# First stage of a convolution and mixture-of-experts kernel: the square root moved behind both product copies, exponentials two batches at a time, the first patches loaded before the stage ends, and half of a normalisation given to VectorE

## The reference, cut to what matters

```python
def branch(x, w, d):                       # four dilations d = 1, 4, 8, 12
    f = softmax(conv3x3(x, w, dilation=d), over the 9 outputs)      # (N, 9, H*W)
    return sum over the 9 taps k of  shifted(x, k, d) * f[k]        # per pixel
n = layernorm over channels of x           # x is (2, 256, 96, 96)
y = conv1x1(concat([n] + [branch(n, w, d) for w, d in ...]), w_proj) + b_proj
x = x + relu(group_norm(y))
t = layernorm(tokens of x)
x = x + t + top-2 mixture of 8 experts on t
```

## Time and profile before

| | us |
|---|---|
| median of 3 runs | 2487.01 (2482.56 to 2492.95) |
| the profiled execution, its own time | 2486.36 |
| its span, first to last instruction | 2484.5 |
| first stage, image 0 and image 1 | 281.9 and 271.6 |
| PE, DVE, ACT, POOL busy over the span | 1950.0, 1626.7, 1274.9, 1058.6 |

### The profile page before, as it was taken

How to read it: one execution, slowest core, us unless ns; L and a number is a source line. 1 busy time by engine, 2 the same in 40 slices (tenths; PEclk the granted TensorE clock), 3 DMA queues, 4 the chain that set the end, 5 groups by cost and what they waited for, 6 DMA issues and landing times.

```text
span 2484.5 us, 60548 instructions
## 1 busy us (share of the span) xinstructions
PE 1950.0 (78%) x20124; PEld 1843.4 (74%) x20125; DVE 1626.7 (65%) x4385; ACT 1274.9 (51%) x2717; POOL 1058.6 (43%) x1444
## 2 busy tenths in 40 slices
PE   4788699999968886999999928723999999993322
PEld 4677599999957775999999927723999999992222
DVE  3465465656555654777887848852788899894653
ACT  4566343333336663556666626512777777771211
POOL 2454412323225543146566614775555555551000
PEclk9999799999989997999999966556999999995555
DMA  5222155566632222677898787743666444446897
GB/s 135 82 77 77 50 177 149 139 173 169 167 107 83 77 64 86 194 208 241 254 269 263 232 277 250 249 162 128 197 207 192 155 159 162 153 157 212 294 302 252
DMA packets 334948, 433.66 MB, mean 175 GB/s; under 512 B 87469, under 2 KB 260141, under 8 KB 333805
## 3 DMA queue, kind: packets, MB, share of 16 engines
q1 hardware_dynamic: 260945, 294.85, 40.3%
q0 software_dynamic: 41024, 97.10, 11.1%
q10 hardware_dynamic: 32784, 39.07, 4.7%
HBM read 277.12 MB, written 159.94 MB: 176 GB/s over the span
## 4 chain that ended last, share of the span: by engine, by line
PE 47%; DMA 16%; DVE 12%; issue 9%; POOL 6%; ACT 6%; SPq 2%; DVEq 2%; POOLq 0%; ACTq 0%
PE ps_y L418 15%; PE ps L418 9%; DMA expert_out<-e_out,dest 6%; PE ps_a L418 6%; PE ps_o L992 6%; POOL expert_in L2204 5%; PE ps_b L929 4%; DMA o_acc<-res_scratch 3%; DMA o_y<-expert_out 3%; DVE stats L1568 2%; PE ps_x L1140 1%; PE ps_tok L831 1%; PE ps_a L875 1%; DVE rows_st L1630 1%; DVE cat_lo L1663 1%
## 5 line engine op out<-in xcount | busy, mean ns | idle before, releaser
L418 PE MATMUL ps_y<-cat_hi,wp 128*128 128x288 f32 x2048 | 473.7, 307 | 1.9 <-DVE cat_lo L1663 1.9
L2227 POOL DMA_INDIRECT expert_out<-e_out,dest x304 | 306.8, 1009 | 233.2 <-DMA expert_out<-e_out,dest 94.4
L2183 POOL DMA_DIRECT2D patches<-rows_scratch x352 | 196.8, 601 | 468.2 <-PE ps_o L979 262.4
L2141 POOL TENSOR_TENSOR taps<-taps,g_rows 96x108 f32<-96x108 f32 (+3 forms) x440 | 236.9, 566 | 271.5 <-ACT g_rows L1241 267.7
L418 PEld LDWEIGHTS ps_y<-cat_hi,wp 128*128 128x128 f32 x2048 | 346.4, 190 | 2.1 <-issue 1.1
L418 PE MATMUL ps_y<-cat_lo,wp 128*128 128x288 f32 x1024 | 303.8, 297 | 0.0
L1309 ACT ACTIVATE bands<-ps_b 112x288 f16<-112x288 f32 (+4 forms) x256 | 105.3, 411 | 342.9 <-PE ps_b L929 333.0
L1663 DVE SCALAR_TENSOR_TENSOR cat_lo<-ps_o,cat_hi 128x288 fp32r<-128x288 f32 (+1 forms) x576 | 227.3, 419 | 63.9 <-ACT cat_hi L1315 59.5
L1315 ACT ACTIVATE cat_hi<-ps_o 128x288 fp32r<-128x288 f32 (+1 forms) x576 | 212.9, 384 | 65.1 <-PE ps_o L979 30.6
L418 PE MATMUL ps<-e_hi,w_now 128*128 128x256 f32 x1216 | 242.6, 282 | 0.6 <-issue 0.2
L1655 DVE SCALAR_TENSOR_TENSOR bands<-ps_b,bands 112x288 f16<-112x288 f32 (+4 forms) x256 | 116.6, 455 | 191.4 <-ACT bands L1309 188.6
(11 more groups left out here) (241 smaller groups left out, 4939.1 us busy)
## 6 DMA issues: line engine op xcount, KB each, us to landing
e_x<-expert_in SPq DMA_DIRECT2D x152, 260.0 KB
o_y<-expert_out SPq DMA_DIRECT2D x48, 768.0 KB, 5.3
patches<-rows_scratch SPq DMA_DIRECT2D x160, 192.0 KB
patches<-rows_scratch SPq DMA_DIRECT2D x256, 108.0 KB
patches<-rows_scratch SPq DMA_DIRECT2D x192, 112.0 KB
x_in<-in_x SPq DMA_DIRECT2D x48, 384.0 KB, 3.2
rows_scratch<-rows_st SPq DMA_DIRECT2D x48, 384.0 KB, 3.0
y_scratch<-y_acc SPq DMA_DIRECT2D x48, 384.0 KB
```

The costliest lines, as they stand in the source:

```text
L418: mm = eng.matmul(out, lhs[p], rhs[q], start=start and n == 0, stop=stop and n == 2)
L2141: last = pool.tensor_tensor(here, here, g_rows[:, u, first:end, i, b:b + nb].rearrange("p r b k -> p r (b k)"), ALU.add)
L2183: pool.dma_start(patch_target(s, n), patch_source(m, s, n)).then_inc(patch_pooled[s % RING], 16)
L2227: pool.indirect_dma_start(out=ys_dram, out_offset=bass.IndirectOffsetOnAxis(ap=at, axis=0), in_=e_out[:, u, j], in_offset=None).then_inc(e ...
```

## The change

In the first stage, on all engines:

1. `deviation(k+2)` stands behind the copies of both taps 0 and 1.
2. The exponentials of batches b-1 and b are run together at the end of the step in which an odd b gets its logits (k = 10, 16, 22), in place in `f_low`. `weights(b-1)` follows in step k+1, `weights(b)` in step k+2, between `statistics` and the second part of `rows_st`; their transposes come one step later still (`weighed_in`, `turned_in`).
3. ACT normalises rows 0 and 1, DVE rows 2 and 3 (new `normalise` on DVE, signal `xn_more`), right after the first part of `rows_st`.
4. After step 23 PE makes both late taps ahead of the own products, with the transposes of batches 4 and 5 behind them.
5. SP and POOL issue the first patches after their last work of the first stage (`free_first_patches` waits until the memory under ring place 0 and the first 16 stored rows are ready).

```diff
+        def weighed_in(k):
+            b = summed_in(k - 1)
+            if b is not None and b % 2 == 1:
+                return b - 1
+            b = summed_in(k - 2)
+            return b if b is not None and b % 2 == 1 else None
         def turned_in(k):
-            return (k - 8) // 3 if k >= 8 and (k - 8) % 3 == 0 else None
+            return weighed_in(k - 1)
...
+        def free_first_patches(eng, m):
+            eng.wait_ge(tok_ready, (m + 1) * GROUPS)
+            eng.wait_ge(ch_ready, (m + 1) * GROUPS)
+            eng.wait_ge(rows_done, (m + 1) * GROUPS)
+            for u in range(2):
+                eng.wait_ge(rows_stored[u], 16 * (m * (GROUPS // 2) + 2))
+            eng.wait_ge(pads_zeroed, 16 * 4 * IMAGES)
...                                          # SP, before it leaves the first stage
+                free_first_patches(sp, m)
+                for n in range(loads(0)):
+                    if not second_queue(0, n):
+                        sp.dma_start(patch_target(0, n), patch_source(m, 0, n)).then_inc(patch_loaded[0], 16)
...                                          # PE
                     pe.wait_ge(xn_done, N + k + 1)
+                    pe.wait_ge(xn_more, N + k + 1)
...
-                late_products(GROUPS - 1)
+                tap_products(GROUPS - 1, 2)
+                tap_products(GROUPS - 1, 3)
+                for o in range(CC):
+                    own_products(GROUPS - 1, o)
+                    turn_filters(BATCHES - 4, o)
+                for o in range(CC):
+                    turn_filters(BATCHES - 3, o)
...                                          # ACT
-                    after(act, f_dve, 3 * (m * BATCHES + b))
-                    act.activation(f_pow[:], f_low[:, b % 2], ACT.Exp).then_inc(f_exp, 1)
+                    act.activation(f_low[:, b % 2], f_low[:, b % 2], ACT.Exp).then_inc(f_exp, 1)
...
                     if k + 1 < GROUPS:
-                        normalise(k + 1, (0, 1))
+                        normalise(k + 1)
                     if k:
                         late_products(k - 1)
-                    if k + 1 < GROUPS:
-                        normalise(k + 1, (2, 3))
                     keep_products(k, 0)
-                    if summed_in(k) is not None:
-                        exponentials(summed_in(k))
+                    keep_products(k, 1)
                     if k + 2 < GROUPS:
                         deviation(k + 2)
-                    keep_products(k, 1)
+                    if summed_in(k) is not None and summed_in(k) % 2 == 1:
+                        exponentials(summed_in(k) - 1)
+                        exponentials(summed_in(k))
...                                          # DVE
+                def normalise(k):
+                    dve.wait_ge(nmr_done, N + k + 1)
+                    for r in range(R // 2, R):
+                        last = dve.tensor_scalar(xn[:, k % 2, r], ps_tok[0:W, k % 2, r], rstd[0:W, k % 2, r:r + 1],
+                                                 nmr[0:W, k % 2, r:r + 1], ALU.mult, ALU.add)
+                    last.then_inc(xn_more, 1)
...
                     dve.wait_ge(xn_done, N + k + 1)
+                    dve.wait_ge(xn_more, N + k + 1)
                     dve.tensor_scalar(rows_st[:, u, :, 0], xn[:, u], SCALE, None, ALU.mult).then_inc(rows_hi_done, 1)
+                    if k + 1 < GROUPS:
+                        normalise(k + 1)
                     if summed_in(k) is not None:
                         lower(summed_in(k))
                     if k + 2 < GROUPS:
                         statistics(k + 2)
+                    if weighed_in(k) is not None:
+                        weights(weighed_in(k))
                     dve.wait_ge(rows_hi_done, N + k + 1)
                     dve.scalar_tensor_tensor(out=rows_st[:, u, :, 1], ...).then_inc(rows_done, 1)
                     if k + 2 < GROUPS:
                         factors(k + 2)
-                    if summed_in(k) is not None:
-                        weights(summed_in(k))
```

More of the change, by code:

```diff
@@ L470, in build @@
                 units += [("tap", m_, k_, 0), ("tap", m_, k_, 1)]
-            late_products(GROUPS - 1)
+            units += [("tap", m_, GROUPS - 1, 2), ("tap", m_, GROUPS - 1, 3)]
+            units += [("own", m_, GROUPS - 1, 0), ("turned", m_, BATCHES - 4, 0), ("own", m_, GROUPS - 1, 1), ("turned", m_, BATCHES - 4, 1)]
+            units += [("turned", m_, BATCHES - 3, 0), ("turned", m_, BATCHES - 3, 1)]
             units += [("logits", m_, BATCHES - 2), ("logits", m_, BATCHES - 1)]
@@ L702, in _ @@
                         kept += 1
-                    load_patches(s)
+                    if s:
+                        load_patches(s)
                     behind = s - UNITS1 - 18
@@ L1230, in normalise @@
                         act.wait_ge(rows_done, N + k - 1)
-                    for r in rows:
+                    for r in range(R // 2):
                         last = act.activation(xn[:, k % 2, r], ps_tok[0:W, k % 2, r], ACT.Identity,
                                               bias=nmr[0:W, k % 2, r:r + 1], scale=rstd[0:W, k % 2, r:r + 1])
-                    if R - 1 in rows:
-                        last.then_inc(xn_done, 1)
+                    last.then_inc(xn_done, 1)
                 def keep_products(k, r):
@@ L1277, in step @@
                     if k + 1 < GROUPS:
-                        normalise(k + 1, (0, 1))
+                        normalise(k + 1)
                     if k:
                         late_products(k - 1)
-                    if k + 1 < GROUPS:
-                        normalise(k + 1, (2, 3))
                     keep_products(k, 0)
-                    if summed_in(k) is not None:
-                        exponentials(summed_in(k))
+                    keep_products(k, 1)
                     if k + 2 < GROUPS:
                         deviation(k + 2)
-                    keep_products(k, 1)
+                    if summed_in(k) is not None and summed_in(k) % 2 == 1:
+                        exponentials(summed_in(k) - 1)
+                        exponentials(summed_in(k))
                 deviation(0)
                 deviation(1)
-                normalise(0, range(R))
+                normalise(0)
                 for k in range(GROUPS):
                     step(k)
-                late_products(GROUPS - 1)
+                keep_products(GROUPS - 1, 2)
+                keep_products(GROUPS - 1, 3)
+                for o in range(CC):
+                    keep_own(GROUPS - 1, o)
+                    keep_filters(BATCHES - 4, o)
+                for o in range(CC):
+                    keep_filters(BATCHES - 3, o)
                 exponentials(BATCHES - 2)
@@ L1642, in _ @@
                     step(k)
+                weights(BATCHES - 3)
                 lower(BATCHES - 2)
@@ L2159, in _ @@
                     add(2, 0, 1).then_inc(taps_added, 1)
+                free_first_patches(pool, m)
+                for n in range(loads(0)):
+                    if second_queue(0, n):
+                        pool.dma_start(patch_target(0, n), patch_source(m, 0, n)).then_inc(patch_pooled[0], 16)
                 leave(pool)
@@ L2177, in _ @@
                 thirds = 0
-                for s in range(STEPS):
+                for s in range(1, STEPS):
                     shared = [n for n in range(loads(s)) if second_queue(s, n)]
```

11 lines of the change are left out of this document (4 added, 7 removed).

## The result

| | before | after |
|---|---|---|
| median of 6 runs, us | 2487.55 (2482.56 to 2494.75) | 2507.75 (2504.77 to 2508.81) |
| the profiled execution, its own time | 2486.36 | 2504.77 |
| its span | 2484.5 | 2502.9 |

The changed kernel takes 1.0077 times as long (95% interval 1.0059 to 1.0096): slower by 0.77%. Forecast were 2493.4 us, a range of 2476 to 2510, and "within 0.5%" as the likeliest case. The time is in the range, 14 us above the value, and on the side (slower by over 0.5%) that I had given 0.23.

The account below looks back on a forecast made before the run. The prediction took a loop of waits between engines, not one engine, as the bound. From 2486.4 us, loop with clock +24.6, behind step 23 -9.0 and patches -8.6 gave 2493.4 us, range 2476 to 2510.

Parts of the forecast that it names:

- within 0.5%: Whole kernel: measured time between 2474.6 and 2499.4 us, hardly told from no change; given 0.65.
- The bound: First stage: no engine bounds it; a loop of waits between engines does, 8.71 us in a plain step.
- The steps without the clock: Loop, steps 7 to 23: +6.3 us an image without clock; steps 10 to 13 about 12.9, 8.8, 12.3, 15.0.
- Late square root, part 3: Loop steps: moving the square root and giving DVE half of the normalisation each change the time by 0.
- `weights`: DVE, steps 11, 12, 17, 18: now inside the loop, delaying `nmr` by 2.69 us each, +10.8 an image.
- The clock: PE behind seven long stalls: clock falls at 1.35 us each, less two before; +6 an image, bounds -2.7 and +16.2.
- two of before: PE in the old loop: clock falls behind two of five double stalls an image, subtracted from the seven expected.
- rival C: PE's products after the seven stalls: clock stays low for most of a step, +20.4, 2513.8 us; chance 0.13.
- Rival B: Loop as forecast, but PE's clock stays up as often as before: 2481.4 us; chance 0.20.
- Behind step 23: End of the first stage: last tap and POOL's additions come earlier, -4.5 us an image, bounds -1.0 and -7.5.
- Patches: Start of the second stage: PE's waits for first patches mostly go, -8.6 us together, bounds 0 and -9.7.
- Rival D: Start of the second stage: prefetch wins nothing, strip 1 being as late as strip 0 was; +8.6, 2502 us; chance 0.05.

Follow-up runs that it names:

- E9: Changed kernel, `weights` ahead of `statistics`, each exponential a step later behind an own-product copy, second part of `rows_st` ahead of `weights` and `statistics`: 2439.87 us, ratio 0.9790 to before.
- E10: Kernel before with parts 3 and 5 and the second part of `rows_st` ahead of the statistics: 2472.11 us, ratio 0.9923.
- E4: Changed kernel with small filler products on PE, whose results nothing reads, in front of each of seven stalls: 2478.83 us, ratio 0.9938 to before.
- E5: Kernel before with part 3 alone, DVE normalising rows 2 and 3: ratio 0.9979.
- E6: Kernel before with part 1 alone, the square root behind the copies of both taps: ratio 1.0066.
- E2: Changed kernel with `weights` ahead of `statistics` on DVE: 2474.64 us, ratio 0.9920 to before.
- E1: Changed kernel with `weights` put back behind `factors` on DVE: 2493.06 us, ratio 0.9990 to before.
- E3: Kernel before with part 5 alone, the first patches issued before the first stage is left: 2482.0 us, ratio 0.9948.
- E7: Kernel before with, from part 4, only both late taps ahead of both own products behind step 23, transposes unchanged: ratio 0.9994.

## Why the prediction was right or wrong

**The bound.** Right: a loop between engines through `nmr`, which the earlier trace rows shows. E9, in which one instruction of that chain was moved and every step became shorter, shows it. I read from the chain that the second part of `rows_st` hides the square root, and not the turn of it, that this part delays `nmr`. E10 shows the limit: with the early square root the same move shortens a plain step by 0.2 us only.

**The steps without the clock.** Right, nearly to the step: forecast 12.9, 8.8, 12.3, 15.0 for steps 10 to 13; E4, with the clock held up, has 12.6, 9.0, 12.1, 14.8. The loop of before holds one fall an image (12.2 for 10.7 us), so 165.4 without it; E4's 171.4 and 171.8 are +6.0 and +6.4, forecast +6.3.

**Late square root, part 3.** 0 each: right for plain steps. E5 shows that part 3 costs nothing. E6 shows that the late square root alone makes the kernel 0.66% slower, so the 0 can hold only with the exponentials moved, which the text did not say.

**`weights`.** Right in mechanism and size (ACT's waits of 2.30 and 3.08 us for `nmr`), as the changed kernel and E2 show. By the earlier trace rows the five instructions end at 148.70, so they take 2.76 us and not 2.69, which changes the term by 0.3. What I did not see is that the old place behind `factors`, measured in E1, is no way out, since transposes and `lower` now need them sooner.

**The clock.** This step failed, in size. "I therefore expect a fall after each of the seven, at 1.35 us, less the two of before: 5 x 1.35 = 6.8, and take 6 since part of a slow stretch will pass while PE stands still." There were six falls in the loop, not seven (the wait in step 23 was only 1.44 us), four at 1.5 to 1.6 us and two at 2.7 to 2.8, because behind the stalls of steps 13 and 19 the clock stayed low twice as long: 11.6 us, less the 1.5 of before, is 10.1 an image where I had 6. The "two of before" were a misreading: by the windows of the single steps the loop of before has one fall in each image (PEclk 0.86 in step 20 of image 0 and step 17 of image 1, 1.00 in all others), so four of the five double stalls passed without one, not three. The price of a fall was read from the one pair of the earlier trace rows, and the long case was put into rival C as all or nothing. Short by 8 us in both images. Rival B is refuted, and C's mechanism held in two of six places.

**Behind step 23.** -4.5 was too much: 30.1 and 30.3 us for 32.9, so -2.7 an image. PE still waited for POOL (1.98 us, 3.91 before), the clock was down, and the logits still took 6.01 us. Short by 3.6 us. This stretch is 31.4 or 31.5 us in E3 with unchanged code, so the size of the gain is uncertain by more than 1 us.

**Patches.** -8.6 forecast, -4.3 and about -4.8 in the profile, shown alone by E3. Rival D is out.

**The rest.** The two terms make 12 us; the profiled execution lies 11.4 over the forecast, and the median 3 over that execution, which was the fastest of the six. "Within 0.5%" had 0.65 though its upper edge was only 6 us away, and the clock term, with bounds of -2.7 and +16.2 in each image, alone reached beyond it.

## What to carry to other kernels

When work is taken off an engine's queue, look at what it is put in front of: here two loads fewer became a wait of PE for a copy. Where PE stands still for 3 to 4 us in one piece, count the clock as well: here six falls cost 11.6 us an image, about as much as ACT's waits for `nmr` (twice 2.30 and 3.08), and filler products that do nothing won them back (22 us of 2505 in the profiles, 1.4% by the ratios). In a loop between engines, move every instruction that nothing waits for out of the stretch between a value's inputs and the value: here one such move won 12 us an image once loads and exponentials were out of the way (E9), and nothing measurable before that (E10).

## What the runs showed of the hardware that was not expected

The same stall doesn't always bring the clock down. Behind the 3.16 us at 145.39 of E1 the next product took 0.83 us, but the same stall one pair later in that execution was followed by a product at full clock:

```profile
214.86 0.51 PE L417 MATMUL ps_a<-wg,xc_hi 128*96 128x324 f32 x2 [3.16 <-ACT g_rows L1270]
226.58 0.67 PE L909 MATMUL ps_ft<-ident,f 96*72 96x96 f16 x6 [2.78 <-DVE f L1656]
```

Nor does a shorter one always leave it up: before has 1.52 and 1.55 us in a row, mostly without a fall, and the same order of work in the loops of E3 and E7 had more falls. So loops of unchanged code differ by 2 us an image from one profiled execution to another, and a gain of that size can't be read from one profile; E9 and E4, without any fall, gave the same 149.5, and 171.4 and 171.8, in both images.

The exponential starts 0.02 us after its table load in the changed kernel too (141.54 + 1.28 against 142.84), so a load costs its 1.28 us and nothing more. Where ACT would be idle anyway it costs almost nothing: in E9 DVE waits 0.41 us for `std` behind the load back to the square root's table, and 0.36 in the steps without a load.

One of the chips ran the kernel before in 2678 us where the others needed 2488 to 2495; the steps of its first stage were the same (8.7 us plain in E5 to E7). What was slow came later: in E7 the second stage of image 1 begins at 974.23 us of the span (before, on the other chip, at 975.74), but its last product with `cat_hi` starts at 1575.8 and not at 1435.7. Why is not known.
